# A four-part graph network on one core: single-bit one-hot codes, and edge messages that VectorE adds itself

## The reference, cut to what matters

```python
x = ln(x + L0(x))   # agg = segment_sum(x[src], dst); relu((x + agg) @ W1 + b1) @ W2 + b2; batch norm; relu
x = ln(x + L1(x))   # agg = segment_sum(x[src], dst); three dense layers, 256 wide inside
x = ln(x + L2(x))   # h = x @ enc_W + enc_b, then 3 times:
                    #   m = relu(cat[h[src], h[dst], edge_features] @ msg_W1[l] + msg_b1[l]) @ msg_W2[l] + msg_b2[l]
                    #   agg = segment_sum(m, dst);  h = gru(agg, h)
x = ln(x + L3(x))   # two GAT layers: e = leaky_relu(a_src.h[src] + a_dst.h[dst]), softmax over the edges of a
                    #   target, out = segment_sum(alpha * h[src], dst) + b
```

## Time and profile before

| | us |
|---|---|
| median of 3 runs | 2476.47 (2474.11 to 2480.77) |
| the profiled execution | 2472.41 |
| its span in the trace | 2470.6 |

### The profile page before, as it was taken

How to read it: one execution, slowest core, us unless ns; L and a number is a source line. 1 busy time by engine, 2 the same in 40 slices (tenths; PEclk the granted TensorE clock), 3 DMA queues, 4 the chain that set the end, 5 groups by cost and what they waited for, 6 DMA issues and landing times. The chain is left out here.

```text
span 2470.6 us, 49093 instructions
## 1 busy us (share of the span) xinstructions
PE 2055.4 (83%) x16085; PEld 1589.4 (64%) x16085; DVE 1758.0 (71%) x6635; ACT 1116.1 (45%) x2756; POOL 1632.6 (66%) x1641
## 2 busy tenths in 40 slices
PE   4878657999799999789999689999679994789961
PEld 3767444878557777447777357777357773577751
DVE  8999954677636888757888568888536777357775
ACT  1333313333232444334434334333448887368883
POOL 5666553777657766577666577767467775777763
PEclk9999865999799999789999799999869997599985
DMA  7989943799417888637888458888146774367751
GB/s 209 296 256 312 273 160 113 254 335 322 136 36 245 286 284 290 196 90 255 288 286 284 143 159 274 289 284 276 46 108 188 217 220 147 63 193 222 224 167 40
DMA packets 308197, 522.97 MB, mean 212 GB/s; under 512 B 105947, under 2 KB 141349, under 8 KB 307748
## 3 DMA queue, kind: packets, MB, share of 16 engines
q1 hardware_dynamic: 236256, 437.07, 52.8%
q0 software_dynamic: 52160, 52.25, 10.4%
q10 hardware_dynamic: 19588, 31.50, 3.6%
HBM read 353.76 MB, written 166.87 MB: 211 GB/s over the span
## 5 line engine op out<-in xcount | busy, mean ns | idle before, releaser
L1837 PE MATMUL ps<-big 128*128 128x256 f16 (+1 forms) x13038 | 1521.5, 276 | 52.5 <-ACT big L834 31.8
L1837 PEld LDWEIGHTS ps<-big 128*128 128x128 fp8e5 x13038 | 1274.9, 99 | 260.8 <-issue 75.6
L745 POOL DMA_INDIRECT ringG<-tab,src_i x1137 | 1113.1, 979 | 445.3 <-issue 325.1
L1270 DVE SCALAR_TENSOR_TENSOR ringG<-ringG,same 128x64 f32<-128x64 f32 x2075 | 578.0, 279 | 80.5 <-ACT ringG L864 52.6
L844 ACT ACTIVATE ringG<-big 128x512 uint8<-128x512 uint8 (+1 forms) x684 | 381.6, 620 | 25.6 <-ACT big L834 0.4
L1270 DVE SCALAR_TENSOR_TENSOR edge_side<-edge_side,same 128x64 f32<-128x64 f32 x1245 | 344.0, 276 | 24.3 <-DMA edge_side<-q_at_start 18.4
L834 ACT ACTIVATE big<-ps 128x512 int32<-128x512 f32 (+1 forms) x228 | 132.9, 583 | 407.9 <-PE ps L1837 407.9
L1242 DVE COPY_PREDICATED ringG<-twins,ringG 128x128 uint32<-128x128 int32 (+2 forms) x798 | 238.8, 299 | 101.8 <-ACT ringG L844 100.8
L1390 DVE SCALAR_TENSOR_TENSOR ringG<-ringG,expo 128x65 f32<-128x65 f32 x830 | 236.9, 285 | 89.7 <-ACT ringG L875 28.3
L745 POOL DMA_INDIRECT ringG<-in_x,src_i x188 | 207.7, 1105 | 129.1 <-DVE ringG L1270 57.8
L864 ACT ACTIVATE ringG<-ringG 128x512 f32<-128x512 f32 x156 | 94.3, 622 | 309.6 <-DVE ringG L1350 309.6
(11 more groups left out here) (276 smaller groups left out, 1602.9 us busy)
## 6 DMA issues: line engine op xcount, KB each, us to landing
big<-kept SPq DMA_DIRECT2D x156, 768.0 KB
sums<-ringG SPq DMA_DIRECT2D x260, 256.0 KB
edge_side<-ef_mix SPq DMA_DIRECT2D x156, 256.0 KB
edge_side<-q_at_start SPq DMA_DIRECT2D x156, 256.0 KB
big<-kept SPq DMA_DIRECT2D x78, 480.0 KB
big<-kept SPq DMA_DIRECT2D x78, 384.0 KB
sums_w<-ringG SPq DMA_DIRECT2D x104, 264.0 KB
kept<-big SPq DMA_DIRECT2D x26, 768.0 KB, 6.2
```

The costliest lines, as they stand in the source:

```text
L745: return pool.indirect_dma_start(out=out_ap, out_offset=None, in_=table, in_offset=bass.IndirectOffsetOnAxis(ap=index, axis=0))
L1270: return v.scalar_tensor_tensor(now, before if u == 0 else source[:, (u - 1) * D:u * D], same[:, c:c + 1], now, ALU.mult, ALU.add)
L1837: mm = pe.matmul(ps[:, m, 0:2 * n] if wide else to, hot[t][:, u * P:(u + 1) * P], opener[:, 0:2 * n] if wide else split[:, t], start=opens ...
```

## The change

Single-bit codes: each of the three edges of a one-hot byte has a bit of its own that is its fp8 value too (mask 0x62 in place of 0x60), `TO_INT` is 32768, and `join_bits` is gone; the tiles of a piece are made after its columns 3 and 5 in place of 5 and 7. Message passes: no identity product on TensorE; VectorE adds `ringQ` to the rows, waiting for `q_filled`, and then the bank; the fill runs one group ahead; SyncE loads a q group when its slot was added (`edge_summed`), one position earlier in its order. In passes 0 and 1 the fetched chunks alternate between two sets of three PSUM banks. In passes 2 to 6 ScalarE copies all chunks of a trip and then spreads them. In pass 0, trip 11's sums stand before the wait for `first_in`.

```diff
-BIT_OF, ODD, MATCHED, SHOWN = (0x01, 0x02, 0x0C), 16, (0x11, 0x22, 0xCC), 0x60606060
-UP_EVEN, UP_ODD = 5, 1
+BIT_OF, ODD, MATCHED, SHOWN = (0x01, 0x10, 0x20), 4, (0x05, 0x50, 0xA0), 0x62626262
+UP_EVEN, DOWN_ODD = 1, 1
-TO_INT = 128.0
+TO_INT = 32768.0
-QAHEAD = 3
+QAHEAD = 1
...
+        def bank_of(k, i, m):
+            return m + CHUNKS * (i % 2) if k < 2 else m
...
             def load_starts(l, g):
                 if g >= QRING:
-                    sp.wait_ge(edge_product, l * NG + g - QRING + 1)
+                    sp.wait_ge(edge_summed, l * NG + g - QRING + 1)
...
-                        if g == 0:
-                            load_starts(l, QRING)
-                        if g + QRING + 1 < NG:
-                            load_starts(l, g + QRING + 1)
+                        if g + QRING < NG:
+                            load_starts(l, g + QRING)
...
+                if k < 2:
+                    for x, m in enumerate(unit.chunks):
+                        copied(x, m)
+                        spread_bytes(x, m)
+                else:
+                    for x, m in enumerate(unit.chunks):
+                        copied(x, m)
+                    for x, m in enumerate(unit.chunks):
+                        spread_bytes(x, m)
...
-            def join_bits(q):
-
-                xs = planes[:, PLANES[q].start:PLANES[q].stop]
-                return chain.mark(v.scalar_tensor_tensor(xs, xs, 2, xs, ALU.logical_shift_right, ALU.bitwise_or))
...
                     v.wait_ge(vchain, taken[0])
+                    v.wait_ge(q_filled, l * NG + g + 1)
+                    link(v.tensor_tensor(rows, rows, ringQ[:, g % QRING], ALU.add))
                     v.wait_ge(edge_product, l * NG + g + 1)
                     v.tensor_tensor(rows, rows, ps[:, EBANK + g % EBANKS, :], ALU.add).then_inc(edge_summed, 1)
...
+            pooled_trip(0, 11)
+
             v.wait_ge(first_in, 48)
...
-            pooled_trip(0, 11)
...
-                                pe.wait_ge(evicted, at(CHUNKS, OPEN + CHUNKS_BEFORE[k] - CHUNKS + m + 1))
+                                pe.wait_ge(evicted, at(CHUNKS, OPEN + CHUNKS_BEFORE[k] - CHUNKS * (2 if k < 2 else 1) + m + 1))
...
-                pe.wait_ge(q_filled, started)
                 settle()
-                pe.matmul(ps[:, EBANK + bank, :], ident[:], ringQ[:, s, :], start=True, stop=False)
                 for u in range(COLS):
                     mm = pe.matmul(ps[:, EBANK + bank, u * D:(u + 1) * D], ringE[:, s, u * P:(u + 1) * P],
-                                   w_e_mix[:, l * D:(l + 1) * D], start=False, stop=(u == COLS - 1))
+                                   w_e_mix[:, l * D:(l + 1) * D], start=True, stop=True)
```

More of the change, by code:

```diff
@@ L419, in parts_of @@
             return home.rearrange("p (u n) -> p u n", u=UMAX)
-        def held(k, m):
-            return ps[:, m] if PASSES[k].width == D else ps[:, 2 * m:2 * m + 2].rearrange("p b n -> p (b n)")
+        def bank_of(k, i, m):
+            return m + CHUNKS * (i % 2) if k < 2 else m
         ef_raw = [edge_side[:, n * EIGHTH:(n + 1) * EIGHTH] for n in range(2)]
@@ L825, in evict, with copied @@
                     act.wait_ge(table_out, 16 * NC * k)
-                for x, m in enumerate(unit.chunks):
-                    us, count = unit.of_chunk(m), CHUNKS_BEFORE[k] + way.before(i) + x + 1
-                    act.wait_ge(chunk_done, count)
+                def copied(x, m):
+                    us = unit.of_chunk(m)
+                    act.wait_ge(chunk_done, CHUNKS_BEFORE[k] + way.before(i) + x + 1)
                     act.wait_ge(placed, CHUNKS_BEFORE[k] + way.before(i))
                     if way.width == D:
-                        of = ps[:, m, us[0] % 2 * n:(us[-1] % 2 + 1) * n].rearrange("p (u n) -> p u n", u=len(us))
+                        of = ps[:, bank_of(k, i, m), us[0] % 2 * n:(us[-1] % 2 + 1) * n].rearrange("p (u n) -> p u n", u=len(us))
                     else:
@@ L834, in evict, with spread_bytes @@
                     nc.scalar.activation(got[:, us[0]:us[-1] + 1], of, ACT.Copy, scale=TO_INT).then_inc(evicted, 1)
-                    js = unit.groups_of(m)
+                def spread_bytes(x, m):
+                    us, js = unit.of_chunk(m), unit.groups_of(m)
                     for j in js:
@@ L839, in evict @@
                         act.wait_ge(summed, k * NG + g + js[-1] - RING + 2)
-                    act.wait_ge(evicted, OPEN + count)
+                    act.wait_ge(evicted, OPEN + CHUNKS_BEFORE[k] + way.before(i) + x + 1)
                     s0, h = slot_of(k, g + js[0]), FULL[js[0]]
@@ L1184, in make_tiles @@
                 if odd:
-                    return v.tensor_scalar(to, of, UP_ODD, SHOWN, ALU.logical_shift_left, ALU.bitwise_and)
+                    return v.tensor_scalar(to, of, DOWN_ODD, SHOWN, ALU.logical_shift_right, ALU.bitwise_and)
                 return v.tensor_scalar(to, of, UP_EVEN, SHOWN, ALU.logical_shift_left, ALU.bitwise_and)
@@ L1204, in make_piece @@
                     matched[3] = keep_matches(q)
-                elif u == (7 if q == 0 else 3):
-                    v.wait_ge(vchain, matched[3])
-                    matched[3] = join_bits(q)
-                    if q == 0:
-                        v.wait_ge(vchain, matched[3])
-                        make_tiles(i, q, 0)
-                        make_tiles(i, q, 1).then_inc(hot_ready, 1)
-                elif u == 5:
+                elif u == 7 and q == 0:
                     v.wait_ge(vchain, matched[3])
                     make_tiles(i, q, 0)
-                elif u == 7:
+                    make_tiles(i, q, 1).then_inc(hot_ready, 1)
+                elif u == 3:
+                    v.wait_ge(vchain, matched[3])
+                    make_tiles(i, q, 0)
+                elif u == 5:
                     make_tiles(i, q, 1).then_inc(hot_ready, 1)
@@ L1831, in fetch_piece @@
                                 if way.width == D:
-                                    to = ps[:, m, u % 2 * n:(u % 2 + 1) * n]
+                                    to = ps[:, bank_of(k, i, m), u % 2 * n:(u % 2 + 1) * n]
                                     opens = t == 0 and u == us[0]
@@ L1836, in fetch_piece @@
                                     to, opens, wide = ps[:, u, 0:n], t == 0, False
-                                mm = pe.matmul(ps[:, m, 0:2 * n] if wide else to, hot[t][:, u * P:(u + 1) * P],
+                                mm = pe.matmul(ps[:, bank_of(k, i, m), 0:2 * n] if wide else to, hot[t][:, u * P:(u + 1) * P],
                                                opener[:, 0:2 * n] if wide else split[:, t], start=opens,
@@ L1856, in fetch_most, with edge_products @@
                         fetch_unit(k, i, trip_in(n, i), PASSES[k].most)
-            def edge_products(l, s, bank, loaded, started, added):
+            def edge_products(l, s, bank, loaded, added):
                 pe.wait_ge(ef_in[s], loaded)
@@ L1875, in single @@
                 def single(g):
-                    edge_products(l, g % ERING, g % EBANKS, 16 * (loads + g // ERING + 1), l * NG + g + 1,
+                    edge_products(l, g % ERING, g % EBANKS, 16 * (loads + g // ERING + 1),
                                   l * NG + g - EBANKS + 1 if g >= EBANKS else None)
```

1 line of the change is left out of this document (removed).

## The result

| | us |
|---|---|
| after, median of 4 runs | 2419.78 (2418.96 to 2421.36) |
| before, median of 4 runs | 2475.84 (2474.11 to 2480.77) |
| ratio | 0.9763, 95% interval 0.975 to 0.9775 |
| after, the profiled execution | 2421.36, span 2419.6 |

A forecast was written before the change was run, and what follows sets the result against it. Bounds: VectorE in pass 0, TensorE in message passes, GpSimd in pass 1 and second GAT, a VectorE-ScalarE loop in first GAT. Savings 38 + 0.7 + 16.8 + 4.3 = 59.8 from 2472.4, plus 4 to the median, 2416; forecast 2415, range 2396 to 2442.

The forecast's parts named there:

- The joining step: Pass 0, VectorE: dropping its 52 instructions saves 39.6 us, less 8 for the DMA queues, so 31.6 us.
- Trip 11: End of pass 0: its sums fall into VectorE's idle before first_d lands; 6.4 us saved, ends 0 and 11.1.
- Two sets of banks: Passes 0 and 1: TensorE no longer waits for ScalarE's copy; 0.7 us saved in pass 1, hidden in pass 0.
- The message passes: TensorE loses the identity product, VectorE gains an addition and sets the pace; 16.8 us saved over three passes.
- The start's loss: Message passes: first sums come later, by 2.6 us in two passes and 0.7 in the third.
- upper bound of 21 us: Message passes: slower by 21 us if the waits beside the added instruction and the later start's cost both went.
- All copies first: ScalarE copies a trip's chunks before spreading: 4 us saved in the first GAT pass, 0.3 in the second.
- The first: Rival: DMA queues bound pass 0, which gives 22 us in place of 38; time 2433, chance 0.22.
- The second: Rival: queues aren't felt and trip 11 fits the idle whole, 39.6 + 11 us in pass 0; 2404, chance 0.15.
- The third: Rival: message passes' added VectorE instruction costs over 0.72 us; 2432 to 2447, chance 0.10, or 2495, chance 0.02.
- The fifth: Rival: VectorE's joins in pass 0 lay in another engine's shadow, as TensorE's, at 19.0 against 18.8 us; no chance given.
- The fourth: Rival: TensorE, now waiting, gets a lower clock in the message passes; 59 us lost, time 2492, chance 0.03.

The follow-up runs named there:

- a: The kernel before with only the single-bit codes, TO_INT and tile steps changed: 2439.96 us, ratio 0.986.
- c: The kernel after with trip 11's sums put back behind the wait for first_in: 2420.39 us, ratio 0.9782.
- b: The kernel before with only the message passes' change, ScalarE's order as before: 2462.79 us, ratio 0.9958.
- e: The kernel after with one set of three PSUM banks in passes 0 and 1: 2416.57 us, ratio 0.9764.
- j: The kernel after with one more VectorE instruction of the same size in each message-pass group: 2529.35 us, ratio 1.0191.
- k: The kernel after with an unused 416-column identity product put back on TensorE in each message-pass group: 2425.61 us, ratio 0.9785.
- h: The kernel after with the fill two groups ahead (QAHEAD = 2): 2420.07 us, ratio 0.9773.
- d: The kernel after with ScalarE's old order (copy a chunk, spread it) in passes 2 to 6 too: 2422.88 us, ratio 0.9794.

## Why the prediction came out right, step by step

The mechanisms of the two large terms were right: the joining step in pass 0, and VectorE in place of TensorE as the bound of the message passes. That the total came within 4 us is in part luck, since errors of both signs cancel: by the means over traces the message passes gave 12.0 and not 16.8, the GAT passes 8.3 and not 4.3, and inside pass 0 two errors of 6 to 8 us met.

*The joining step* was forecast at 39.6 us with 8 taken back by the DMA queues, 31.6. From the first `keep_matches` to the first sum it gave 5.5 (a: 6.0; forecast 6.7, but VectorE then waits 0.88 us for ScalarE's first spread), in ten trips 28.1 (forecast 29.9), in trip 10 nothing: 33.6. The 8 us for the queues were wrong: the share stayed at 0.97 with 349 in place of 313 GB/s, and the trips were won. And trip 10 was counted as if VectorE still set its end; from the store of `first_d` on, SyncE and GpSimd do.

*Trip 11*: forecast 6.4, measured about 4.6 by the table in c. The mechanism named (gathers of trip 12 close behind) was right; what holds the gathers, SyncE's own wait for `first_d` ahead of the stores of sums, was not seen, although it stands in SyncE's order. With what the stretch lost beside it (table in c), pass 0 comes to 33.6 + 2.7 = 36.3 us, as the means say.

*Two sets of banks*: forecast 0.7, all in pass 1. Over all traces pass 1 takes 247.3 to 248.3 us with one set (before, a, b, e) and 244.8 to 247.1 with two (ten kernels), 1.6 us between the means: more than forecast, too little to show in e's time.

*The message passes*: the mechanism, VectorE's loop in place of TensorE's, was right and is shown by j; k shows how close behind TensorE stands. The start's loss was forecast at 2.6 us; the second addition came 17.5 us after the pass's first gather before and 20.1 after, 2.6 later. The mis-sized term is the loop. There were 37 with twins and 13 without, as counted, but they take 5.27 and 4.51 us, not 5.24 and 4.46: from L1352 to L1354 it is 0.72 to 0.79 us by the starts, 0.745 in the mean, not the 0.72 taken from the earlier trace rows. That is 1.8 us a pass. TensorE's own trip was mis-sized the other way, which cost nothing: where it runs ahead without a wait, four groups take 759.90 - 742.27 = 17.6 us and not 18.2, so the product had held it for (21.3 - 17.6) / 4 = 0.9 us a group and not the 0.75 taken.

```profile
742.27 0.40 PE L1870 MATMUL ps<-w_e_mix,edge_side 128*128 128x64 bf16 x8
...
759.90 0.40 PE L1870 MATMUL ps<-w_e_mix,edge_side 128*128 128x64 bf16 x8
```

Of VectorE's 1.8 us some 1.0 goes with the fill one ahead: in h, two ahead, the loops without a wait are 5.26 and 4.46. In the third pass VectorE waited 4.1 us for gathers ahead of the first addition, and its gain was 2.4, not 4.5. The prediction's upper bound of 21 us for this term should have been 22.7 by its own numbers (16.8 and the start's loss of 2.6 + 2.6 + 0.7); nothing hung on it. It also expected TensorE to wait for `edge_summed` or `evicted`: from 740 to 940 us it waits 18.3 us in 12 pieces for its one-hot tiles (`big<-kept`), and 0.6 for ScalarE.

*All copies first*: forecast 4.3 in the GAT passes, by the two traces 6.3, by d 7.7 and 3.0, by the means 6.8 and 1.5, so it was priced too low by about half. No row gives the 0.37 us a trip of the forecast; the trip does fall by nearly that, from 18.42 to 18.05. The first copy of a trip on ScalarE, and the same in the next trip, before (L834) and now (L832):

```profile
1924.89 0.61 ACT L834 ACTIVATE big<-ps 128x528 int32<-128x528 f32 x1
...
1943.31 0.60 ACT L834 ACTIVATE big<-ps 128x528 int32<-128x528 f32 x1
```

```profile
1861.81 1.57 ACT L832 ACTIVATE big<-ps 128x528 int32<-128x528 f32 x3
...
1879.86 1.58 ACT L832 ACTIVATE big<-ps 128x528 int32<-128x528 f32 x3
```

Thirteen trips give 13 x 0.37 = 4.8 us; what the rest of the 8.3 is was not looked into.

*The rivals.* The first (queues bound pass 0) is refuted by the trips of 19.2 us and by a. The second was too high, since neither the joining step (33.6 of 39.6) nor trip 11 (4.6 of 11) was won whole. The third, that the new addition is held: it takes 0.69 to 0.76 us in all 156 cases, refuted. The Trainium skill (SBUF — State Buffer, "Who interferes with whom") has a VectorE instruction with two SBUF inputs contend with a GpSimd instruction that reads SBUF. Nothing of it is seen at these additions, and none of the 573 gathers of the message passes took longer than 1.45 us. It may be what is seen at the end of pass 0, where two gathers took 2.17 and 3.98 us beside the two long VectorE instructions at 297.05 and 298.98, as in the earlier trace rows; no run separates it from another cause. The fifth, that TensorE bounds pass 0, came near: it is busy 23.90 of 25 us there, and the trips of 19.2 us are 0.4 above the 18.8 worked out for VectorE, but VectorE shows no wait of over 0.1 us from 53 to 275 us.

The fourth, the clock, needs the pass by stretches. The kernel after, first message pass, columns as in the windows above:

```profile
740.00:940.00 200.00, 180.90 (x1804) 157.40 (x1802) 195.72 (x796) 85.45 (x159) 144.59 (x144) 0.98 0.89 294
940.00:980.00 40.00, 26.86 (x266) 22.49 (x263) 39.27 (x160) 10.20 (x20) 30.56 (x32) 0.84 0.83 268
980.00:996.00 16.00, 0.59 (x8) 0.46 (x8) 15.68 (x62) 5.86 (x11) 2.54 (x3) 0.50 0.32 106
```

Over 200 us with waits of up to 2.7 us the granted clock was 0.98 (0.99 in the other two passes; 1.00 before), near the 1.00 forecast. The mean of a pass fell from 0.98 to 0.92, 0.94 and 0.93 because of its end: TensorE's work runs out, the clock goes to 0.84 and at last to 0.50, its level of 1.2 GHz, and VectorE is busy 39.27 of 40 and 15.68 of 16 us all the same. So the fall of the mean is not the one that the rival asks for, and VectorE's loops show no cost of it.

## What to carry to other kernels

Price a saved instruction by the distance to the next start in its own stretch, and only up to the point from which another chain sets the end; that point may be a wait in an issuing queue's order, far from the engine one looks at. A DMA busy share near one is not a ceiling: look for a stretch where the same share carried more bytes. Where one engine's loop has become the bound, more slack elsewhere (here a second set of banks, an earlier first spread) brings nothing that shows, and how far ahead a buffer is filled has to be changed together with the place of its load in the issuing order: one of these alone cost 445 us here. A start made earlier is kept only if what feeds the next trips comes earlier too. And read a mean granted clock by stretches before it is held against a kernel: the end of a pass, where TensorE has no work left, pulls it down for nothing.

## What was not expected of the hardware

The same 0.97 of DMA share went with 313 GB/s before and 349 after over the same 25 us of pass 0, and a share of 1.04 with 394 from 50 to 62 us in the kernel after. It went with far less, too: from 266 to 276 us, while SyncE waits for the store of `first_d` (12.5 KB), the share is 0.98 and the queues move 70 GB/s. The kernels with the same pass 0 ended it anywhere in 319.0 to 322.8 us, so a single trace does not tell effects of 3 us there. Whether a faster store of `first_d` would let the end of pass 0 move stays open; that was not tried.
